# A Mamba-2 block between two feed-forward halves: the held output goes over ScalarE and PSUM, e rows load ahead of the cum rows, x ring of seven

## What is computed

```python
proj = hidden_states @ in_proj_w                  # gate, x, B, C, dt
hbc = silu(causal depthwise conv of 4 taps over x, B, C)
dt = softplus(dt + dt_bias); cum = cumsum(dt * A) within a chunk
decay = exp(cum_i - cum_j) for i >= j
Y_diag = (C B^T * decay * dt_j) @ x               # within a chunk
states = sum over the chunk of decay_to_end * dt * B x^T
new = chunk_decay * prev + states                 # scan over chunks
Y_off = (C @ prev_states) * exp(cum)              # exp(cum) is the e row
yr = Y_diag + Y_off + D_param * x
hidden = rmsnorm(yr * silu(gate)) * norm_w
return hidden @ out_proj_w                        # 4096 -> 256
```

## Time and profile before

| | us |
|---|---|
| median of 3 runs | 1471.52 (1467.57 to 1472.78) |
| the profiled execution | 1473.38 |
| its span | 1471.7 |
| TensorE busy | 1333.7 (91%) |
| VectorE busy | 1191.9 (81%) |
| ScalarE busy | 1007.0 (68%) |
| GpSimd busy | 820.3 (56%) |

### The profile page before, as it was taken

How to read it: one execution, slowest core, us unless ns; L and a number is a source line. 1 busy time by engine, 2 the same in 40 slices (tenths; PEclk the granted TensorE clock), 3 DMA queues, 4 the chain that set the end, 5 groups by cost and what they waited for, 6 DMA issues and landing times. The chain is left out here.

```text
span 1471.7 us, 27111 instructions
## 1 busy us (share of the span) xinstructions
PE 1333.7 (91%) x8896; PEld 1134.4 (77%) x8896; DVE 1191.9 (81%) x2643; ACT 1007.0 (68%) x2067; POOL 820.3 (56%) x896
## 2 busy tenths in 40 slices
PE   5889887767999999999999999999999999986998
PEld 4778766556888878888888888888888888864887
DVE  5753433676999999999999999999999999986433
ACT  1114433667889988888988898888899888861332
POOL 1004211004678777878877787797787878681000
PEclk9999998988999999999999999999999999996999
DMA  6221000222444444453444444444444444334000
GB/s 128 66 86 36 15 6 10 58 65 73 125 111 98 126 117 109 119 115 98 119 128 108 117 105 116 116 122 117 112 104 120 123 110 116 94 80 185 15 14 29
DMA packets 102085, 136.43 MB, mean 93 GB/s; under 512 B 27744, under 2 KB 49856, under 8 KB 101824
## 3 DMA queue, kind: packets, MB, share of 16 engines
q1 hardware_dynamic: 99840, 132.67, 34.4%
q10 hardware_dynamic: 2112, 2.10, 0.4%
HBM read 124.76 MB, written 9.96 MB: 92 GB/s over the span
## 5 line engine op out<-in xcount | busy, mean ns | idle before, releaser
L845 ACT ACTIVATE M<-cum_row,cum_table 128x128 f32<-128x128 f32 x1024 | 312.1, 390 | 0.0
L1272 DVE SCALAR_TENSOR_TENSOR xs<-psum,conv_w_sb,xs 128x509 f32<-128x509 f32 (+2 forms) x384 | 283.2, 738 | 0.4
L985 POOL TENSOR_TENSOR hid_lo<-hid,hid_hi 128x512 fp32r<-128x512 f32 x128 | 196.2, 1533 | 67.3 <-PE psum L40 61.5
L1060 POOL TENSOR_TENSOR hid<-hid,sg 128x512 f32<-128x512 f32 x128 | 165.5, 1293 | 94.0 <-DVE hid L1340 93.9
L1049 POOL TENSOR_TENSOR squares<-squares,sq 128x512 f32<-128x512 f32 x124 | 160.0, 1290 | 75.3 <-ACT sq L822 75.3
L1299 DVE TENSOR_TENSOR M<-M,CB 128x1024 f32<-128x1024 f32 x128 | 183.5, 1434 | 0.0
L1655 PE MATMUL psum<-M,xdt 128*64 128x128 f32 x2048 | 140.1, 278 | 24.3 <-DVE psum L1331 24.2
L827 ACT ACTIVATE sg<-psum 128x512 f32<-128x512 f32 x128 | 75.1, 587 | 104.5 <-PE psum L40 96.9
L1655 PEld LDWEIGHTS psum<-M,xdt 128*64 128x64 f32 x2048 | 110.1, 136 | 47.2 <-DVE M L1299 27.4
L1632 PE MATMUL psum<-xend,B_tok 128*128 128x128 f32 x1024 | 140.1, 281 | 2.5 <-DVE carry L1323 2.4
L853 ACT ACTIVATE M<-M 128x1024 f32<-128x1024 f32 x128 | 134.5, 1051 | 0.5
(11 more groups left out here) (210 smaller groups left out, 3422.0 us busy)
## 6 DMA issues: line engine op xcount, KB each, us to landing
cum_row<-cum_scratch SPq DMA_DIRECT2D x256, 256.0 KB, 4.4
e_row<-e_scratch SPq DMA_DIRECT2D x256, 128.0 KB, 3.4
xw_raw<-L_attn_in_proj_w_dram SPq DMA_DIRECT2D x32, 128.0 KB, 3.3
wo_raw<-L_attn_out_proj_w_dram SPq DMA_DIRECT2D x32, 128.0 KB, 3.0
gw_raw<-L_attn_in_proj_w_dram SPq DMA_DIRECT2D x16, 256.0 KB, 4.5
x_res<-_attn_hidden_states_dram ACTq DMA_DIRECT2D x4, 512.0 KB, 9.4
x_scratch<-x_res SPq DMA_DIRECT2D x4, 512.0 KB, 2.6
x_res<-x_scratch SPq DMA_DIRECT2D x1, 2048.0 KB, 8.0
```

The lines of the kernel that those rows point to most:

```text
L845: last = nc.scalar.activation(M[:, v % 3, h, c * CH:(c + 1) * CH], cum_row[:, v % 2, h, c * CH:(c + 1) * CH], ACT.Relu, bias=scalar_of(CUM ...
L985: nc.gpsimd.tensor_tensor(hid_lo[:], hid[:, v % 2, :], hid_hi[:, v % 2, :].bitcast(F32), ALU.subtract).then_inc(hid_lo_done, 1)
L1060: nc.gpsimd.tensor_tensor(hid[:, v % 2, :], hid[:, v % 2, :], sg[:, v % 8, :], ALU.mult).then_inc(hid_done, 1)
L1272: nc.vector.scalar_tensor_tensor(xs[:, v % 8, shift:], psum[:, X_BANK + v % 2, 0:TT - shift], tap_of(v, step), xs[:, v % 8, shift:], ALU.m ...
```

## The change

Four edits:

1. `add_out` on VectorE is gone. ScalarE gets `take_out`: at the start of each phase slot, after the square, two copies from banks 6 and 7 into `mixed`. From slot 16 on it then does `put_back`: two copies of the held sums of the new tile from `mixed` into the banks. The out projection then never begins with `start=True` after the first group: it accumulates on what was put back, and waits for `out_begun`.
2. `e_row` has two buffers, with a semaphore each; `load_e` waits for the scaling two slots back, and stands ahead of `load_cum` in SyncE's order.
3. The ring `xs` has 7 places instead of 8; `evac_x(v)` waits for the skip path of v - 7.
4. Three functions on GpSimd that were defined a second time (or not called) are removed.

```diff
-    xs = sb("xs", [P, 8, TT], F32)
+    xs = sb("xs", [P, 7, TT], F32)
-    e_row = sb("e_row", [P, TT], F32)
+    e_row = sb("e_row", [P, 2, TT], F32)
...
             def load_e(v):
                 head = 2 * pair_of(v)
-                sp.wait_ge(off_scaled, nth(v - 1))
+                sp.wait_ge(off_scaled, nth(v - 2))
...
+                if alive(s + 3):
+                    load_e(s + 3)
                 if alive(s + 5):
                     load_cum(s + 5)
-                if alive(s + 3):
-                    load_e(s + 3)
...
             def evac_x(v):
 
                 act.wait_ge(x_proj, nth(v))
-                act.wait_ge(v_done, nth(v - 8))
+                act.wait_ge(v_done, nth(v - 7))
...
+            def take_out(v):
+
+                t = at_slot(v)[1]
+                act.wait_ge(out_done, nth(v))
+                if v == GP - 1:
+                    act.wait_ge(cum_out, 16 * 2 * NT)
+                for m in range(KT):
+                    nc.scalar.activation(mixed[:, m, tile(t)], psum[:, OUT_BANK + m, :], ACT.Copy).then_inc(mixed_done, 1)
+
+            def put_back(v):
+
+                if not SLOTS <= v < ALL:
+                    return
+                t = at_slot(v)[1]
+                act.wait_ge(mixed_done, KT * (v // GP))
+                for m in range(KT):
+                    nc.scalar.activation(psum[:, OUT_BANK + m, :], mixed[:, m, tile(t)], ACT.Copy).then_inc(out_begun, 1)
...
                 if alive(s):
                     square(s)
+                if s > 0 and s % GP == 0:
+                    take_out(s - 1)
+                    put_back(s)
...
+            take_out(ALL - 1)
...
             def scale_off(v):
                 dve.wait_ge(off_done, nth(v))
-                dve.wait_ge(e_in, (v + 1) * 32)
+                dve.wait_ge(e_in[v % 2], (v // 2 + 1) * 32)
...
-            def add_out(v):
-
-                j, t = at_slot(v)
-                dve.wait_ge(out_done, nth(v))
-                if v == GP - 1:
-                    dve.wait_ge(cum_out, 16 * 2 * NT)
-                for m in range(KT):
-                    if v < SLOTS:
-                        nc.vector.tensor_copy(mixed[:, m, tile(t)], psum[:, OUT_BANK + m, :]).then_inc(mixed_done, 1)
-                    else:
-                        nc.vector.tensor_tensor(mixed[:, m, tile(t)], psum[:, OUT_BANK + m, :], mixed[:, m, tile(t)],
-                                                ALU.add).then_inc(mixed_done, 1)
...
-                if s >= 0 and s % GP == GP - 1:
-                    add_out(s)
...
                 if j == 0:
                     pe.wait_ge(mixed_done, KT * (v // GP))
+                    if v >= SLOTS:
+                        pe.wait_ge(out_begun, KT * (v // GP - NT + 1))
                 for m in range(KT):
                     cols = slice(m * P, (m + 1) * P)
                     last = split_matmul(nc, psum[:, OUT_BANK + m, :], wo_hi[:, j, cols], wo_lo[:, j, cols],
-                                        hid_hi[:, v % 2, :], hid_lo[:], start=(j == 0), stop=(j == GP - 1))
+                                        hid_hi[:, v % 2, :], hid_lo[:], start=(j == 0 and v < SLOTS),
+                                        stop=(j == GP - 1), skip=(v >= SLOTS))
```

More of the change, by code:

```diff
@@ L467, in macaron @@
     cum_in, xw_in, wo_in = [[sem(f"{n}{i}") for i in range(2)] for n in ("cum_in", "xw_in", "wo_in")]
-    e_in, gw_in = sem("e_in"), sem("gw_in")
+    e_in, gw_in = [sem(f"e_in{i}") for i in range(2)], sem("gw_in")
     halo_in, halo_step, halo_done = sem("halo_in"), sem("halo_step"), sem("halo_done")
-    folded = sem("folded")
+    folded, out_begun = sem("folded"), sem("out_begun")
     wo_hi_done, wo_lo_done, hid_hi_done, hid_lo_done = [sem(n) for n in ("wo_hi_done", "wo_lo_done", "hid_hi_done", "hid_lo_done")]
@@ L618, in load_e @@
                 head = 2 * pair_of(v)
-                sp.wait_ge(off_scaled, nth(v - 1))
+                sp.wait_ge(off_scaled, nth(v - 2))
                 for h in range(2):
-                    sp.dma_start(e_row[h * HP:(h + 1) * HP, :],
+                    sp.dma_start(e_row[h * HP:(h + 1) * HP, v % 2, :],
                                  e_dram[head + h:head + h + 1, tile(at_slot(v)[1])].partition_broadcast(HP)
-                                 .rearrange("p o t -> p (o t)")).then_inc(e_in, 16)
+                                 .rearrange("p o t -> p (o t)")).then_inc(e_in[v % 2], 16)
             for p in range(2):
@@ L835, in silu_x @@
                 act.wait_ge(conv_done, nth(v))
-                nc.scalar.activation(xs[:, v % 8, :], xs[:, v % 8, :], ACT.Silu).then_inc(xs_done, 1)
+                nc.scalar.activation(xs[:, v % 7, :], xs[:, v % 7, :], ACT.Silu).then_inc(xs_done, 1)
             def relus(v):
@@ L857, in evac_x @@
                 act.wait_ge(x_proj, nth(v))
-                act.wait_ge(v_done, nth(v - 8))
-                nc.scalar.activation(xs[:, v % 8, :], bank(X_BANK + v % 2), ACT.Identity,
+                act.wait_ge(v_done, nth(v - 7))
+                nc.scalar.activation(xs[:, v % 7, :], bank(X_BANK + v % 2), ACT.Identity,
                                      bias=conv_b_sb[:, pair_of(v):pair_of(v) + 1],
                                      scale=tap_of(v, TAPS - 1)).then_inc(x_evac, 1)
+            def take_out(v):
[12 more added lines that the diff above has]
+                    nc.scalar.activation(psum[:, OUT_BANK + m, :], mixed[:, m, tile(t)], ACT.Copy).then_inc(out_begun, 1)
             for g in range(NT):
@@ L1009, in split_wo @@
                 split_wo_lo(p)
[L1011 to L1041, removed]
             def add_squares(v):
@@ L1267, in conv_tap @@
                         dve.wait_ge(halo_done, sums_before(v))
-                        nc.vector.scalar_tensor_tensor(xs[:, v % 8, 0:shift], psum[:, X_BANK + v % 2, 0:shift],
+                        nc.vector.scalar_tensor_tensor(xs[:, v % 7, 0:shift], psum[:, X_BANK + v % 2, 0:shift],
                                                        tap_of(v, TAPS - 1), halo_sum[:, t % 2, j, :], ALU.mult, ALU.add)
@@ L1271, in conv_tap @@
                     dve.wait_ge(conv_step, 2 * v + step)
-                nc.vector.scalar_tensor_tensor(xs[:, v % 8, shift:], psum[:, X_BANK + v % 2, 0:TT - shift], tap_of(v, step),
-                                               xs[:, v % 8, shift:], ALU.mult, ALU.add).then_inc(
+                nc.vector.scalar_tensor_tensor(xs[:, v % 7, shift:], psum[:, X_BANK + v % 2, 0:TT - shift], tap_of(v, step),
+                                               xs[:, v % 7, shift:], ALU.mult, ALU.add).then_inc(
                                                    conv_done if step == TAPS - 2 else conv_step, 1)
@@ L1328, in scale_off @@
                 dve.wait_ge(off_done, nth(v))
-                dve.wait_ge(e_in, (v + 1) * 32)
+                dve.wait_ge(e_in[v % 2], (v // 2 + 1) * 32)
                 cols = slice(CH if at_slot(v)[1] == 0 else 0, TT)
-                nc.vector.tensor_tensor(psum[:, Y_BANK, cols], psum[:, Y_BANK, cols], e_row[:, cols],
+                nc.vector.tensor_tensor(psum[:, Y_BANK, cols], psum[:, Y_BANK, cols], e_row[:, v % 2, cols],
                                         ALU.mult).then_inc(off_scaled, 1)
@@ L1339, in skip_path @@
                 p = pair_of(v)
-                nc.vector.scalar_tensor_tensor(hid[:, v % 2, :], xs[:, v % 8, :], d_sb[:, p:p + 1], bank(Y_BANK),
+                nc.vector.scalar_tensor_tensor(hid[:, v % 2, :], xs[:, v % 7, :], d_sb[:, p:p + 1], bank(Y_BANK),
                                                ALU.mult, ALU.add).then_inc(v_done, 1)
-            def add_out(v):
-                j, t = at_slot(v)
-                dve.wait_ge(out_done, nth(v))
-                if v == GP - 1:
-                    dve.wait_ge(cum_out, 16 * 2 * NT)
-                for m in range(KT):
-                    if v < SLOTS:
-                        nc.vector.tensor_copy(mixed[:, m, tile(t)], psum[:, OUT_BANK + m, :]).then_inc(mixed_done, 1)
-                    else:
-                        nc.vector.tensor_tensor(mixed[:, m, tile(t)], psum[:, OUT_BANK + m, :], mixed[:, m, tile(t)],
-                                                ALU.add).then_inc(mixed_done, 1)
             dve.wait_ge(lut_in, 16)
@@ L1620, in turn_x @@
                 for c in range(CPT):
-                    last = nc.tensor.transpose(psum[:, XT_BANK, c * P:(c + 1) * P], xs[:, v % 8, c * CH:(c + 1) * CH], ident[:])
+                    last = nc.tensor.transpose(psum[:, XT_BANK, c * P:(c + 1) * P], xs[:, v % 7, c * CH:(c + 1) * CH], ident[:])
                 last.then_inc(x_turned, 1)
```

## The result

The changed kernel takes **1511.8 us** (median of 4 runs, 1510.6 to 1512.7) against 1472.2 for the kernel before beside it: a ratio of **1.0269 (1.0251 to 1.0287)**, 39.6 us slower. Forecast were 1488 us and a range of 1468 to 1502: the direction was right, and the forecast was +16 us where +39.6 were measured.

The account below looks back on a forecast made before the run. TensorE's own work and its waits bound the loop, with ScalarE's gapless phase deciding. Groups 1 to 6 +19.8, e waits -2.0, group 0 -0.3, group 7 -0.5, last slots -1.2: +15.8, so 1488 us, range 1468 to 1502.

Parts of the forecast that it names:

- the fours: The slot loop cut into stretches of four slots, each from a phase slot; TensorE's floors 29.97 to 30.36 us.
- ScalarE's phase: ScalarE's gapless 16.07 us from the phase slot's square to the second x evacuation; the copies go to its head.
- Part 1, S: Time that ScalarE's four copies add per phase: 2.1 us, bounds 1.9 and 2.6, no table load for Copy.
- Parts 2 to 5: VectorE relieved of 1.20 us every fourth slot; early e saves 2.7; seven x places free; out projection covered by 3.
- Chain B: ScalarE's square through GpSimd's `gw_lo` to TensorE's gate projection: the copies' lateness comes through, +1.9 us each time.
- kind 8: The four slots beginning at slot 8 of each group of 16: 32.44 us before, forecast +1.9.
- Chain A: Phase square, x evacuation, VectorE's slot (6.63), e scaling, TensorE's diagonal matmuls, next square: 31.4 us per four slots.
- Kinds 0 and 12: Four-slot stretches beginning at slots 0 and 12 of 16: 31.05 and 29.97 us before, forecast +0.35 and +1.2.
- R3: Slower still, some 1500 us: copies into PSUM at 0.76, or mask product meeting GpSimd in more slots; chance 0.12.
- kind 4: The four slots beginning at slot 4 of each group of 16: 31.64 us before, forecast -0.2.
- R2: Faster, some 1448 us: waits for VectorE go and ScalarE's lateness is absorbed; chance 0.13.
- R1: Within 0.5%, some 1478 us: the GpSimd path swallows more of the copies' lateness, +6 us in all; chance 0.20.

Follow-up runs that it names:

- Experiment 2: Changed kernel with 14 extra 512-column matmuls on TensorE during its wait for `gw_lo` in slot 10 of each group: 1499.2 us, ratio 1.0178.
- experiment 4: Changed kernel with ScalarE's silus moved to slots 2 mod 4, copies left in place: 1442.5 us, ratio 0.9812; same move on the kernel before: 1494.1 us.

## Why the forecast was wrong

**The reading of what bounds it**, the fours, their floors and ScalarE's phase as the place of decision: right. Moving the gate split, or the silus away from the copies, changed the time as the chains said (1476.1 for about 1478, 1442.5 for 1438 to 1450).

**Part 1, S.** Forecast 2.1, measured 2.14, no table load: right. The Trainium skill's faster way into PSUM ("ScalarE: Activation LUTs", Step-by-step: what each stage is for) doesn't show: two copies into PSUM last 1.12, two out of it 1.07, and the silus from SBUF to SBUF of the earlier trace rows some 1.14 for two; the measurement decides.

**Parts 2 to 5.** VectorE's relief, the ring of seven and the cover of the out projection: right as far as seen, TensorE has no wait on the copies in the loop and evacuations none on the skip path. e: 3 us, taken as 2.7. What I had not seen is that its worth depends on where the silus stand.

**Chain B in kind 8** failed, and it is most of the error: +12.2 forecast, +27.5 measured. The step is the price "+1.9": S comes straight through to the length of the four, and what TensorE does after a longer wait was put at nothing, without a reason. The wait itself came as said (0.8 to 3.8, "3 or 4 us" in the text). But behind it TensorE's clock is at 1.2 GHz, 1.00 to 0.50 in the rows, and 7 to 13 matmuls are slower. Experiment 2 isolates it: 12.6 us over seven waits, 1.8 each, and in kind 8 alone 14.7 of the 15.3 us that it cost beyond the forecast. The 0.79 to 0.91 us waits of before had left the clock at 1.00, and I priced a wait of another length by them. The Trainium skill ("TensorE: Matmul & The Clock Gate", Part 1) has this: an idle array falls to half its clock and comes back only under work. The case agrees in both levels, with the fall up to 0.7 us behind the wait in group 1. That sentence belonged among the rivals, and I left it out although the text foresaw a wait of nearly 4 us. It also explains group 0: there the copies are half, and I gave kind 8 +0.8; TensorE waited 2.98, its clock fell there too, 13 matmuls lasted 0.20 us longer (2.6 us), and it cost +3.7.

**Chain A** was mis-sized in the length of VectorE's slot. Kinds 0 and 12 together cost 8.4 us more than forecast, of 24 us missed. Measured at slot 80, from the square at 995.38:

```profile
1012.82 0.76 ACT L859 ACTIVATE xs<-psum,conv_b_sb,conv_w_sb 128x512 f32<-128x512 f32 x1
```

```profile
1013.61 0.16 DVE L1254 COPY halo<-psum 128x3 f32<-128x3 f32 x1 [2.17 <-ACT xs L859]
1013.69 0.21 DVE L1258 SCALAR_TENSOR_TENSOR xs<-psum,conv_w_sb,halo_sum 128x3 f32<-128x3 f32 x1
...
1019.17 1.69 DVE L1289 TENSOR_TENSOR M<-M,CB 128x1024 f32<-128x1024 f32 x1
1020.79 0.69 DVE L1321 TENSOR_TENSOR psum<-psum,e_row 128x512 f32<-128x512 f32 x1
```

18.2 from the square to the end of the evacuation (forecast 18.2), and VectorE's slot **7.18 where I took 6.63**. Of the 0.55, 0.41 is the mask product: it takes 1.62 of the queue there (1019.17 to 1020.79), and 1.21 in the slot that the forecast read. The rest is a tap of three columns (1013.69) that the forecast's slot doesn't have. GpSimd is at work on `hid` from 1018.52 to 1019.78, so 0.61 us of it are left when the product begins. The Trainium skill ("SBUF — State Buffer", Who interferes with whom) lets a VectorE instruction with two SBUF inputs and a GpSimd one that reads SBUF exclude each other, the later one waiting for the whole of the earlier. The traces agree, and give the size: in those before and after, a mask product that begins with r us of a GpSimd instruction left lasts 1.08 + r, at least 1.21 (125 of 126 cases), and all others last 1.21 to 1.23. When the product is first GpSimd is the longer one, as with the squares of 1.98 above. The meeting comes in every four of kinds 0 and 12 from group 1 on (products of 1.68 to 1.75). I had written that the meeting might come in more slots, and gave it to R3 as a tail. The four closes on itself as computed: 18.2 + 7.2 + 0.8 + 5.7 = 32.0 between squares, 32.2 between states groups. Kind 0 got +7.5 in all for +1.8, kind 12 +10.0 for +7.3, kind 4 -3.8 for -4.6.

**The rivals.** R2 was dead by the same phase that was read, and experiment 4 is its mirror: taken out of the gapless stretch the same copies are absorbed. That its 1442.5 us lie near R2's 1448 is luck, since it is another kernel. R1 needed chain B to swallow more; it swallowed less. R3 had the right direction and one cause of the two right: the mask product met GpSimd in more slots, which is most of the 8.4 us of chain A. Its other cause, slow copies into PSUM, didn't come, and the clock it didn't have either. A range made of S and the length of VectorE's slot can't hold a term that is missing.

**Not settled.** Why the clock falls within the wait in some groups and after it in others, and so stays low for 7 to 13 matmuls. And how the value of the early e divides between its place in the queue and the second buffer.

## What to carry to other kernels

Work moved to an engine with time to spare isn't free if its time lies elsewhere: find the stretch in which that engine runs without a gap, follow it to who waits for its end, and put the new work outside it. When a forecast makes a wait longer, price what the waiting engine does after it too: behind TensorE's waits of 0.8 us the clock was still 2.4 GHz, behind those of 3.8 it was halved, and 1.8 us more were lost. And one edit's worth holds for one schedule: here `add_out` on ScalarE costs 43 us or saves some 25, and the early e rows save 3 us or 14 and more, by the slot in which the silus stand.

## What the runs showed of the hardware

- TensorE's granted clock was 1.00 through waits of 0.70 to 0.91 us. It fell to 0.50 (1.2 GHz) during waits of 2.98 and 3.82 us, or up to 0.7 us after one of 3.84; 512-column matmuls were then 0.43 us apart instead of 0.23, 7 to 13 of them. Fourteen dummy matmuls in the wait kept it at 1.00 and saved 1.8 us each time.
- A float32 mask product of 128x1024 with two inputs in SBUF took VectorE 1.21 us, and 1.08 us plus the time left where GpSimd was in the middle of an instruction, up to 2.2 us. A GpSimd `squares` of 128x512 that began during it took 1.8 to 2.05 us for 1.27.
- ScalarE writes PSUM from SBUF at the price of its other copies: two in 1.12 us of 512 columns, two from PSUM in 1.07.
- Matmuls that accumulate on a bank that ScalarE has written start 0.23 us apart as others do (932.53 and on in slot 72 of the changed kernel).
